# Attention output by transfers in token order, and the values' product ahead of a round's first T scores, in a one-core decoder layer

## What is computed

```
x = x + attn(layernorm(x))       # 16 heads of 16, causal softmax
x = x + mlstm(layernorm(x), ctx) # 8 heads of 32, gated matrix memory
x = x + moe(layernorm(x))        # 8 experts, top 2, 256 -> 1024 -> 256
```

## Time and profile before

| | us |
|---|---|
| median of 3 runs | 965.46 |
| lowest, highest | 962.29, 969.97 |
| profiled execution: its time | 962.93 |
| profiled execution: its span | 961.2 |

### The profile page before, as it was taken

How to read it: one execution, slowest core, us unless ns; L and a number is a source line. 1 busy time by engine, 2 the same in 40 slices (tenths; PEclk the granted TensorE clock), 3 DMA queues, 4 the chain that set the end, 5 groups by cost and what they waited for, 6 DMA issues and landing times.

```text
span 961.2 us, 31757 instructions
## 1 busy us (share of the span) xinstructions
PE 887.1 (92%) x11966; PEld 653.0 (68%) x11966; DVE 586.2 (61%) x1292; ACT 487.4 (51%) x839; POOL 496.3 (52%) x705
## 2 busy tenths in 40 slices
PE   5999999999997689899998988999999999999995
PEld 3667667667665356565564776778888888878783
DVE  4856766766764456777777657455555555555552
ACT  3667677677666367566455542333333333333331
POOL 2556666566565333366666667534444434444432
PEclk9999999999999799999888899999999999999998
DMA  9222443443445654455453233433332333233322
GB/s 283 70 57 67 93 129 90 96 127 90 92 119 121 172 183 132 146 177 179 144 162 118 90 86 89 87 62 51 48 51 47 53 49 52 46 52 52 47 34 23
DMA packets 133197, 92.96 MB, mean 97 GB/s; under 512 B 75712, under 2 KB 114112, under 8 KB 132928
## 3 DMA queue, kind: packets, MB, share of 16 engines
q1 hardware_dynamic: 119760, 73.10, 28.2%
q0 software_dynamic: 13296, 17.83, 11.1%
HBM read 54.65 MB, written 37.32 MB: 96 GB/s over the span
## 4 chain that ended last, share of the span: by engine, by line
PE 80%; DVE 7%; ACT 5%; issue 3%; DMA 2%; SPq 2%; another core or an unknown queue 1%; POOL 0%; DVEq 0%; ACTq 0%; POOLq 0%
PE pair L933 19%; PE pair L949 12%; PE pair L951 6%; PE pair L634 5%; PE pair L671 5%; PE pair L657 4%; PE pair L811 3%; PE pair L607 3%; PE pair L684 2%; PE pair L825 2%; PE pair L829 2%; PE pair L861 2%; PE pair L900 2%; PE pair L786 1%; PE pair L837 1%
## 5 line engine op out<-in xcount | busy, mean ns | idle before, releaser
L933 PE MATMUL pair<-XTs,WU 128*128 128x128 bf16 x3408 | 283.9, 219 | 5.9 <-DVE XTs L1269 2.9
L933 PEld LDWEIGHTS pair<-XTs,WU 128*128 x3408 | 238.1, 98 | 71.7 <-issue 8.7
L1603 POOL DMA_INDIRECT out_d<-XB x71 | 116.1, 1635 | 207.4 <-DVE XB L1291 174.0
L949 PE MATMUL pair<-WD,Hh 128*128 x568 | 214.8, 379 | 1.3 <-issue 1.3
L1469 ACT ACTIVATE Hf<-pair 128x512 f32<-128x512 f32 x142 | 84.8, 597 | 219.5 <-PE pair L933 207.9
L1282 DVE CAST Hh<-Hf 128x512 bf16<-128x512 f32 x142 | 64.5, 454 | 172.1 <-ACT Hf L1469 166.9
L951 PE MATMUL pair<-WD,Hl 128*128 x568 | 154.7, 272 | 0.0
L1284 DVE TENSOR_TENSOR Hl<-Hf,Hh 128x512 bf16<-128x512 f32 x142 | 99.5, 701 | 4.9
L1514 POOL TENSOR_SCALAR_AFFINE_SELECT PT<-PT 128x512 f32<-128x512 f32 (+1 forms) x96 | 73.9, 787 | 44.2 <-ACT PT L1320 28.7
L1576 POOL DMA_INDIRECT xs_scr<-XB,WGf x64 | 66.9, 1045 | 31.7 <-issue 18.2
L1488 POOL TENSOR_TENSOR LS<-LS,mhalf 128x2 f32<-128x2 f32 x48 | 34.1, 711 | 94.6 <-DVE LS L976 93.9
(11 more groups left out here) (243 smaller groups left out, 1728.9 us busy)
## 6 DMA issues: line engine op xcount, KB each, us to landing
XB<-xs_scr SPq DMA_DIRECT2D x71, 130.0 KB
STG<-wup_in SPq DMA_DIRECT2D x32, 256.0 KB
q_scr<-SPL SPq DMA_DIRECT2D x16, 512.0 KB, 4.2
STG<-wdn_in SPq DMA_DIRECT2D x32, 256.0 KB
o_scr<-On SPq DMA_DIRECT2D x32, 128.0 KB, 4.2
Mm<-o_scr SPq DMA_DIRECT2D x16, 256.0 KB, 3.0
CnT<-ctxt_in SPq DMA_DIRECT2D x16, 256.0 KB, 4.0
CX<-ctx_in SPq DMA_DIRECT2D x16, 256.0 KB, 4.4
```

What stands on the lines that cost most here:

```text
L933: t = e.matmul(upb(j, k)[:, 128 * (fm % 4):128 * (fm % 4) + 128], WU[:, bass.ds(reg[j] * 4096 + off, 128)], XTs[:, r, hx, dk, :], start=n ...
L949: e.matmul(yb[r][:, 0:512], Hh[:, r, hsl], WD[:, bass.ds(reg[i] * 4096 + 512 * fk, 512)], start=fk == 0, stop=False, skip_group_check=True)
L1603: e.indirect_dma_start(out=out, out_offset=bass.IndirectOffsetOnAxis(ap=XS[:, i % NX, 256:257].bitcast(I32), axis=0), in_=Yf[:, i % NY, :] ...
```

## The change

- `OTs` is written by ACT in another order (token groups outside), with a strided read of PSUM. The heads are placed in another order in the weights, so that a transfer can take out what belongs together.
- A4 and the transposes of `Mm` on TensorE are gone. SP moves `OTs` to DRAM in token order in four transfers (word OT), takes the sums to `dnc` (128 x 32) by another, and reads the result back to `XA` (XA).
- DVE's RC takes the reciprocals and multiplies with `wsq` (128 x 32 each); SP writes the factors to DRAM in four transfers (WB) and reads them back spread over 16 partitions each (BC, two transfers) into the single buffer `XR`.
- DVE's X1 multiplies `XA` by `XR` and adds it to x (two operations of 128 x 512).
- On TensorE `PV:2` stands ahead of `T0:1:0`. ACT's T0 word moves to match.
- SP's words have a new order: the loads of the chunks stand at the end of the round. POOL's A6s stands between the masks of T0.
- SP waits that are new: OT for RC of the batch before; XA for OT's four transfers and X1 of two batches before; WB for RC of the same batch; BC for WB's transfers and X1 of the batch before.

```diff
 ROUND = {
-    "tensor": "AX:1 MG:1 S1:0:0 T0:1:0 PV:2 S1:0:1 QK:-1 T0:1:1 S0:0 VX:0 T2:1 GT:15 weights:1:2 A4:2",
-    "vector": "Gp:16 weights:-2:0 A6s:4 weights:-1:1 S1:0:1 S0:0 VX:0 A4:2 weights:1:2 MG:0 AX:0 S1:-1:0 Gs:15 A0s:-3",
-    "scalar": "PV:2 A0n:-2 QK:-1 T0:1:1 Gt:13 A6c:4 weights:-2:0 A6n:4 VX:0 T2:1 weights:-1:1 AX:0 GT:15 MG:0 T0:0:0",
-    "gpsimd": "weights:0:2 split:0 T0:1:0 T0:1:1 split:0 GT:15 T2:1 A6c:4 A0s:-3 A6s:3",
-    "sync": "GT:15 load:0 A4:3 AX:1 Go:16 queries:16 decays:16",
+    "tensor": "AX:1 MG:1 S1:0:0 PV:2 T0:1:0 S1:0:1 QK:-1 T0:1:1 S0:0 VX:0 T2:1 GT:15 weights:1:2",
+    "vector": "Gp:16 weights:-2:0 weights:-1:1 S1:0:1 X1:4 A6s:4 S0:0 RC:2 weights:1:2 MG:0 AX:0 S1:-1:0 Gs:15 A0s:-3",
+    "scalar": "PV:2 T0:1:0 A0n:-2 QK:-1 T0:1:1 Gt:13 A6c:4 weights:-2:0 A6n:4 VX:0 T2:1 weights:-1:1 AX:0 GT:15 MG:0",
+    "gpsimd": "weights:0:2 split:0 T0:1:0 A6s:4 T0:1:1 split:0 GT:15 T2:1 A6c:4 A0s:-3",
+    "sync": "GT:15 BC:3 AX:1 OT:2 WB:2 XA:2 load:0:0 load:0:1 Go:16 queries:16 decays:16",
 }
...
+        def vector_denominators(e, w, b):
+            w.wait_ge(l_dc, 16 * (b + 1))
+            w.wait_ge(l_wb, 64 * b)
+            e.reciprocal(dnc[:, :], dnc[:, :]).then_inc(dvc.sem, dvc.up())
+            w.wait_ge(dvc.sem, dvc.n)
+            e.tensor_tensor(rc[:, :], dnc[:, :], wsq[:, :], ALU.mult).then_inc(rc_.sem, 1)
+
+        def vector_residual(e, w, b):
+            r = b % 2
+            w.wait_ge(l_xa[r], 16 * (b // 2 + 1))
+            w.wait_ge(l_bc, 32 * (b + 1))
+            e.tensor_tensor(XA[:, r, :, :], XA[:, r, :, :], XR[:, :, :], ALU.mult).then_inc(dvc.sem, dvc.up())
+            w.wait_ge(dvc.sem, dvc.n)
+            e.tensor_tensor(xb(b), XA[:, r, :, :], xb(b), ALU.add).then_inc(x1_.sem, 1)
...
-                    w.wait_ge(wsq_, 2)
-                    w.wait_ge(oT.sem, oT.at(b - 1))
-                    e.activation(OTs[:, :, :], pair_of("PV", b)[:, :, :].rearrange("p a (r c) -> p (a r) c", r=2), ACT.Copy).then_inc(ot_.sem, 1)
+                    w.wait_ge(wsq_, 1)
+                    w.wait_ge(l_ot, 64 * b)
+                    w.wait_ge(l_dc, 16 * b)
+                    e.activation(OTs[:, :, :].rearrange("p g c -> p (g c)").rearrange("p (s g d) -> p s g d", s=16, g=4),
+                                 pair_of("PV", b)[:, :, :].rearrange("p a (r d s) -> p s (a r) d", r=2, s=16), ACT.Copy).then_inc(ot_.sem, 1)
...
-                elif kind == "A4":
-                    w.wait_ge(on_.sem, on_.at(b))
+                elif kind == "OT":
+                    w.wait_ge(ot_.sem, ot_.at(b))
+                    w.wait_ge(rc_.sem, rc_.at(b - 1))
+                    e.dma_start(dnc[:, :], OTs[16:128:32, :, :].rearrange("p g c -> p (g c)").rearrange("p (s c) -> p s c", c=32)).then_inc(l_dc, 16)
+                    ov = osc[b, :].rearrange("(s h d) -> h s d", s=16, h=16)
+                    for j in range(4):
+                        e.dma_start(ov[:, :, 64 * j:64 * j + 64], OTs[32 * j:32 * j + 16, :, :].rearrange("p g c -> p (g c)").rearrange(
+                            "p (s c) -> p s c", s=16)).then_inc(l_ot, 16)
+                elif kind == "XA":
+                    w.wait_ge(l_ot, 64 * (b + 1))
+                    w.wait_ge(x1_.sem, x1_.at(b - 2))
+                    e.dma_start(XA[:, b % 2, :, :], osc[b, :].rearrange("(t p d) -> p t d", t=2, p=128)).then_inc(l_xa[b % 2], 16)
+                elif kind == "WB":
+                    w.wait_ge(rc_.sem, rc_.at(b))
+                    for j in range(4):
+                        e.dma_start(rsc[b, :].rearrange("(s j k c) -> j s k c", s=16, j=4, k=2)[j], rc[32 * j:32 * j + 32, :]).then_inc(l_wb, 16)
+                elif kind == "BC":
+                    w.wait_ge(l_wb, 64 * (b + 1))
+                    w.wait_ge(x1_.sem, x1_.at(b - 1))
                     for tt in range(2):
-                        e.dma_start(osc[b, :].rearrange("(n t p h) -> t p n h", n=NH, t=2, h=16)[tt], On[:, tt, :, :]).then_inc(l_o, 16)
-                    if b < B - 1:
-                        merged(e, w, b)
+                        e.dma_start(XR[:, tt, :], rsc[b, 2048 * tt:2048 * tt + 2048].rearrange("(s a d) -> s a d", s=8, a=1).broadcast_to(
+                            [8, 16, 256])).then_inc(l_bc, 16)
```

More of the change, by code:

```diff
@@ L115, in attn_steps @@
     yield "MG", B + 1, 0
-    yield "A4", B - 1, 0
+    yield "OT", B - 1, 0
     yield "contexts", 0, 0
+    yield "queries", 1, 0
+    yield "WB", B - 1, 0
+    yield "XA", B - 1, 0
     yield "decays", 1, 0
-    yield "queries", 1, 0
     yield "contexts", 1, 0
+    yield "BC", B - 1, 0
 def attention_rest():
     z = B - 1
-    return {(0, 0): (("A6s", z - 2), ("Mm", z), ("X1", z - 1), ("A6n", z - 2), ("A6c", z - 2)),
+    return {(0, 0): (("X1", z - 2), ("A6s", z - 2), ("RC", z), ("X1", z - 1), ("A6n", z - 2), ("A6c", z - 2)),
             (0, 1): (("A6s", z - 1), ("XQ", z - 2), ("A6n", z - 1), ("A6c", z - 1)), (0, 2): (("X1", z), ("A6s", z)),
@@ L281, in build @@
         OTs = sb("OTs", [128, 4, 256], F32, ca)
[L282 to L285, removed]
+        dnc = sb("dnc", [128, 32], F32, ca)
+        rc = sb("rc", [128, 32], F32, ca)
+        wsq = sb("wsq", [128, 32], F32, ca)
+        XA = sb("XA", [128, 2, 2, 256], F32, ca)
+        XR = sb("XR", [128, 2, 256], F32, ca)
         QN = sb("QN", [128, 2, 256], F32, ca)
@@ L394, in build @@
         t2m, ex2, pt2 = (sig(n, [(b, u) for b, _ in of(pe_attn, "T2") for u in range(2)]) for n in ("t2m", "ex2", "pt2"))
-        pv, ot_, oT, on_, mT, x1_ = (sig(n, each) for n in ("pv", "ot_", "oT", "on_", "mT", "x1_"))
-        l_o, l_m = sem("l_o"), [sem("l_m0"), sem("l_m1")]
+        pv, ot_, rc_, x1_ = (sig(n, each) for n in ("pv", "ot_", "rc_", "x1_"))
+        l_ot, l_dc, l_wb, l_bc, l_xa = sem("l_ot"), sem("l_dc"), sem("l_wb"), sem("l_bc"), [sem("l_xa0"), sem("l_xa1")]
         qn_, qT, qnh, qnl, ch_, cl_ = (sig(n, each) for n in ("qn_", "qT", "qnh", "qnl", "ch_", "cl_"))
@@ L519, in build @@
         EPS = 5e-5
[L522 removed]
+        tb_users = [s[:2] for s in pe_steps if s[0] in ("XQ", "GA", "GT", "GE", "B4", "B5")]
         def tb_free(w, kind, b):
@@ L529, in tb_free @@
             kind, b = tb_users[i - 1]
-            if kind == "X1":
-                w.wait_ge(x1_.sem, x1_.at(b))
-            elif kind == "XQ":
+            if kind == "XQ":
                 w.wait_ge(qnl.sem, qnl.at(b))
@@ L677, in tensor_attn @@
                     ps = pair_of("VX", b)
[L678 to L690, removed]
-                        for dk in range(2):
[L692 to L703, removed]
+                    w.wait_ge(wql, 2)
+                    for tt in range(2):
+                        n = 0
+                        for dk in range(2):
+                            for wt, v in ((WQh, xTh), (WQl, xTh), (WQh, xTl)):
+                                t = e.matmul(ps[:, 0, 256 * tt:256 * tt + 256], v[:, b % 2, dk, 128 * tt:128 * tt + 128], wt[:, dk, 512:768],
+                                             start=n == 0, stop=n == 5, skip_group_check=True)
+                                n += 1
+                    t.then_inc(vmm.sem, 1)
                 elif kind == "AX":
@@ L1828, in constants @@
     c[:, C_U:C_U + 128] = p[:, None] < p[None, :]
-    for tt in range(2):
-        for s in range(16):
-            c[:, C_SEL + 16 * tt + s] = s == 8 * tt + p // 16
+    for k in range(8):
+        c[:, C_SEL + k] = 2 * (p // 32) + p % 2 == k
     c[:, C_M0] = p % 32 < 16
@@ L1852, in layout @@
     w = i["L0_attn_W_qkv"].transpose(1, 2, 0).reshape(D, 3, 16, 16).transpose(0, 1, 3, 2)
+    places = [4 * j + 2 * a + r for a in range(2) for j in range(4) for r in range(2)]
+    w = np.concatenate([w[:, 0:2][:, :, places], w[:, 2:3]], 1)
     wq = w.reshape(2, 128, 768).transpose(1, 0, 2)
```

68 lines of the change are left out of this document (21 added, 47 removed).

## The result

| | before | after |
|---|---|---|
| median of 4 runs, us | 963.88 | 1177.6 |
| lowest, highest | 961.58, 969.97 | 1174.27, 1183.7 |
| profiled span | 961.2 | 1178.8 |
| mean granted clock | 0.967 | 0.866 |
| PV of batch 0 | 46.60 | 43.48 |

The account below looks back on a forecast made before the run. TensorE's own work bounded the kernel before. Twelve rounds of 30.8 us and two of 29.0 against 249.1 give +178.5; less the earlier start and tail, +175 on 962.93, 1138, plus 2.5 for the median: 1140, range 1100 to 1190.

Parts of the forecast that it names:

- The ring: PV, S0, X1, BC, OT, RC, WB, XA, load, POOL's split and masks, next PV: 30.8 us in each of 12 rounds.
- the 0.8 for the clock: TensorE's low clock after standing still, added to each of the 12 longer rounds: 0.8 us, bounds 0 and 4.
- Rounds 2 and 3: Attention rounds without X1 or A6s in the way: 27.1 us plus 1.9 for slow clock, 29.0 each.
- I take -2: From PV of batch 14 on: TensorE's removed transposes against four transfers in a row before X1 of batch 15, net -2 us.
- from the mLSTM on nothing but the start differs: Sign expected in the profile after: the mLSTM part changes only in when it starts.
- start: First PV of the attention stage comes 1.3 us earlier, because T0 stands behind it.
- Removed work, worth nothing: TensorE's removed A4 and `Mm` transposes, 1.46 us a round, save nothing because TensorE waits anyway.
- Rival 1: Loads don't hold POOL, so only the removed TensorE work counts: faster, 943 us; chance 0.08.
- 16.3 to 16.7 us, if nothing else became late: Length of an attention round with TensorE's 1.46 us of removed work gone, from 17.8 before.
- the last 2.2 us to `xTl`: End of the long round: from T2's exps' end on ScalarE to `xTl`, which releases PV's banks, 2.2 us.
- Rival 2: X1 is no detour on SP's way to OT, all 14 rounds 28.5 us on average: 1112 us; chance 0.09.
- Rival 3: TensorE's clock stays low, its work takes twice as long, rounds 33.5 and 31 us: 1177 us; chance 0.10.
- PV ahead of T0: TensorE's new order: T0 stands between PV and S1's maxima and takes 1.3 us of the round.

Follow-up runs that it names:

- run 1: Kernel after, with SP's two chunk loads moved from the end of its round to the front, ahead of BC: 1029.16 us, ratio 1.0626 to before.
- run 3: Kernel after, SP untouched, with POOL's two splits moved from ahead of the masks to the end of its round: 1035.42 us, ratio 1.0680 to before.
- run 7: Kernel after, with 58 unread matmuls added on TensorE ahead of AX's transposes in 11 rounds: 1176.84 us, ratio 1.2229 to before.
- run 8: Kernel after, with SP's order loads, AX, Go, queries, decays, OT, BC, WB, XA: 970.09 us, ratio 1.0107 to before.
- run 10: Kernel of run 9, with BC of batch 15 issued ahead of the last batch's decays and contexts: 967.22 us, ratio 1.0022 to before.
- run 4: Kernel before, with only PV put ahead of T0 on TensorE and ACT's T0 word moved to match: 972.19 us, ratio 1.0107 to before.
- run 9: Kernel of run 8, with T0 put back ahead of PV on TensorE and ACT's order put back too: 970.84 us, ratio 1.0056 to before.
- run 6: Kernel after, with SP's loads first and AX's issues (queries out, context in) also ahead of BC: 973.34 us, ratio 1.0104 to before.
- run 5: Kernel after, loads left in place, with BC moved from the front of SP's round to between OT and WB: 1160.16 us, ratio 1.1967 to before.
- run 2: Kernel after, with SP's two loads moved between OT and WB, still behind BC: 1117.39 us, ratio 1.1525 to before.

## Why the prediction was right, and where it was not

**The ring: right, but for one link.** The links up to the square roots are in the chain of after, in the order given; runs 1 and 3 break it from two sides. From there to `xTl` the prediction went over VX's copy and T2's exps on ScalarE. The chain goes over AX's transposes and the gates' sums on TensorE (L700 to L745), at clock 0.50, and only by a little. ScalarE's time line has the exps' chain end 0.58 us before VectorE's pieces start at 327.02:

```profile
325.84 0.60 ACT L1378 ACTIVATE SPL<-pair 128x512 bf16<-128x512 f32 x1
```

With the clock kept up (run 7) the exps' chain is the later one. The ring's length by steps, in us after PV (predicted, measured at 295.90):

| step | predicted | measured |
|---|---|---|
| X1 done, BC issued | 9.2 | 9.4 |
| `dnc` issued | 11.0 | 11.7 |
| `dnc` landed | 14.0 | 15.5 |
| RC done | 14.6 | 16.1 |
| load issued | 17.0 | 19.2 |
| load landed | 20.0 | 22.3 |
| QN may start | 24.3 | 26.7 |
| next PV | 30.8 | 32.4 |

**Mis-sized terms of the ring.** The issues: BC's two took 1.31 us and WB's four 2.48, 0.6 each, where I priced all at the 0.47 of a queries' issue; together +1.3 from X1 to the load. `dnc` landed after 3.73, not 3.0. X1's two operations took 1.33, not 1.8, and the slow clock at PV's start put S1's maxima at +8.0 instead of 7.4, so that 0.6 of the 0.8 for the clock was already spent by then. These errors go both ways, and part of the nearness of 30.8 to 32.4 is that they cancel. Twelve rings of 32.6 instead of 30.8 are 21.4 of the 21.6 us that the rounds missed by. Rounds 2 and 3 took 28.2 and 30.0 (predicted 29.0 each).

**The tail: wrong, the larger error for its size.** "I take -2" measured +20.6. The step counted TensorE's removed transposes and one chain of four transfers, and not that each word of SP in the last rounds stands ahead of the mLSTM's own transfers; the prediction's "from the mLSTM on nothing but the start differs" failed with it. With both rings open and the mLSTM's words ahead (run 8) the tail is still 8.6 above before; run 10 takes 2.2 more away. So SP's order is shown for some 14 us of it. The rest is open; PV's move alone, with the old order of SP, gave 7.0 (run 4), but putting T0 first again (run 9) gave nothing back.

**Sum.** Predicted +175.2 in the span, measured +217.6; the difference is 21.6 (rounds) + 22.6 (tail) - 1.8 (start, -3.1 instead of -1.3).

**Removed work, worth nothing: right in the kernel as it is. Rival 1's price: wrong.** It said that with the loads out of the way the time would be 943. Run 1 reaches 1029, run 6 973, run 8 970. It missed the second ring (context behind BC), and it took all of 1.46 a round off the chain. In fact 0.76 a round came out with T0 first (18.11 to 17.35), and the same with PV first (run 4's 18.35 to run 8's 17.59). `Mm`'s 0.44 stood ahead of T2's scores, and if it came out whole, only some 0.3 of A4's 1.02 did: the rest had been covering ScalarE's chain from T2's exps on. The sentence "16.3 to 16.7 us, if nothing else became late" is that error: TensorE's group on the chain is no price as long as another chain of almost the same length ends beside it. Its signs were the 0.73 of idle time in the earlier trace rows and the exps' end at 239.67, from which the prediction itself counted the last 2.2 us to `xTl`.

**Rival 2** (X1 no detour, 1112): half right, 1160 in run 5. **Rival 3** (clock, 1177): the time came, the reason did not (run 7).

**PV ahead of T0** was priced with the ring alone; by run 4 it costs 0.24 a round when TensorE bounds the round.

**Left open.** A second buffer for `XR` should cut BC's wait for X1; it was not tried. Nor were these transfers on another engine's queue, which the runs suggest most. What makes up the last 6 us of the tail (671.9 in run 10 against 665.5) wasn't found either.

## What to carry to other kernels

In an in-order queue a word costs what everything behind it waits: before a word that waits for this round's compute is put ahead of others, list each one behind it and who is first to need it. Opening one ring shows the next; here the loads hid the context. And before work is counted as saved, look at the short idle time that ends it: if a second chain is less than the saving away, only that distance comes out (here about half of 1.46).

## What was not expected of the hardware

**TensorE's clock fell out of dense work.** In run 7, after 11.02 busy of 12 us at clock 1.00 and one pause of 1.08 us, the clock was 0.50 two microseconds later, in some rounds and not in others. The kernel before pauses 0.73 us in each round and stays at 1.00, and so does run 8, which pauses 1.08 in each (clock 1.00 from 60 to 280): the length of that pause doesn't decide it. The Trainium skill (TensorE: Matmul & The Clock Gate, "A second HAM failure mode: psum-queue depth-cycling") tells of a kernel whose short idle times between groups of matmuls let the clock swing between its two levels. Run 7 shows such swings, run 8 doesn't, and no run here tells what decides it.

**Issues differ in price, and not with their bytes.** On SP's queue a broadcast read of `XR` took 0.64, a write of 4 KB from 32 partitions in WB 0.59, the context of 256 KB 0.43, a load of 256 KB 0.47 (0.94 for two). Nor is it the shape alone: `dnc`'s read of 4 partitions took 0.94 to 1.03 where the context had been issued directly ahead of it (after, runs 1, 2 and 7), and 0.56 to 0.63 in runs 5, 6 and 8 to 10.

**VectorE waits out GpSimd's instruction.** RC's product over 128x32 takes 0.19 us alone. In run 8, VectorE's time line and then GpSimd's:

```profile
214.81 1.20 DVE L988 TENSOR_TENSOR rc<-dnc,wsq 128x32 f32<-128x32 f32 x1
```

```profile
214.80 1.17 POOL L1481 TENSOR_TENSOR WU<-STG,WU 128x512 bf16<-128x512 f32 x1
```

It ends with GpSimd's instruction, which began 0.01 earlier. X1's first operation likewise takes 0.68 in after, where POOL stands still, and up to 1.56 in run 3, there beside a split's 1.16. The Trainium skill (SBUF — State Buffer, "Who interferes with whom") says that a VectorE instruction with two inputs in SBUF contends with a GpSimd instruction that reads SBUF. The trace agrees: here VectorE's waited for the one that had begun first. A kernel that puts such operations in place of ones that read PSUM, as this change does with X1 and RC, takes on this wait.
